# A recurrence whose candidate is summed by one scan in PSUM, and a transformer block whose norms are made tile by tile

## The reference

```
x = x + topk_mask(fside, cond, x)
x = x + small_attention(x, cond)
x = x + gru(cond, x)          # 512 steps, state 4 x 512
x = x + dit_block(x, cond)    # per batch of 4

def cell(h, x):
    gi = x @ W_ih + b_ih;  gh = h @ W_hh + b_hh
    r = sigmoid(i_r + h_r);  z = sigmoid(i_z + h_z)
    n = tanh(i_n + r * h_n)
    return (1 - z) * n + z * h

def dit_block(x, c):
    shift1, scale1, gate1, shift2, scale2, gate2 = split(c @ ada_w + ada_b)
    x1 = ln(x) * (1 + scale1) + shift1
    x = x + gate1 * (attention(x1) @ out_w + out_b)      # 16 heads of 128
    x2 = ln(x) * (1 + scale2) + shift2
    return x + gate2 * (gelu(x2 @ w1 + b1) @ w2 + b2)    # hidden 2048
```

## Time and profile before

| | |
|---|---|
| median of 3 runs | 4443.78 us (4442.07 to 4444.65) |
| the profiled execution | 4447.41 us, span 4445.7 us |
| TensorE busy | 3784.4 us (85%), 69948 matmuls |
| weight loads | 2814.5 us (63%) |
| VectorE busy | 2845.6 us (64%) |
| ScalarE busy | 2080.4 us (47%) |
| GpSimd busy | 517.7 us (12%) |

### The profile page before, as it was taken

One profiled execution on the slowest core, in us unless ns is written; L12 is line 12 of the kernel. 1 busy time (PEld: TensorE's weight loads), 2 busy tenths in 40 slices (PEclk: granted clock), 3 DMA queues, 4 the chain that ended last, 5 costly groups with the idle time before them and its releaser, 6 DMA issues. The chain is left out here.

```text
span 4445.7 us, 180216 instructions
## 1 busy us (share of the span) xinstructions
PE 3784.4 (85%) x69948; PEld 2814.5 (63%) x69948; DVE 2845.6 (64%) x11557; ACT 2080.4 (47%) x7520; POOL 517.7 (12%) x425
## 2 busy tenths in 40 slices
PE   1526766776999999999999996998799889988997
PEld 1424453543489999999999993564356436633653
DVE  7877787786677777777777773574267226623752
ACT  2015574665755555555555551453145215422532
POOL 3005374471000000000000000001000100010001
PEclk9999998998955555555555557999899989998999
DMA  2002131232000000000000006110221122022102
GB/s 85 0 24 67 49 115 40 77 98 69 0 6 6 6 6 6 6 6 6 6 6 6 6 6 238 67 38 38 109 76 29 62 106 65 20 80 114 46 12 85
DMA packets 114616, 209.71 MB, mean 47 GB/s; under 512 B 44154, under 2 KB 76922, under 8 KB 112000
## 3 DMA queue, kind: packets, MB, share of 16 engines
q1 hardware_dynamic: 114436, 207.35, 13.7%
HBM read 165.35 MB, written 33.57 MB: 45 GB/s over the span
## 5 line engine op out<-in xcount | busy, mean ns | idle before, releaser
L497 ACT ACTIVATE dit_prob<-dit_bank,dit_head_nbias 128x512 f32<-128x512 f32 x256 | 176.0, 688 | 350.7 <-DVE dit_head_nbias L515 350.3
L1272 PE MATMUL gru_sum_na<-gru_state_parts,w_hh_lo 128*128 128x4 f16 x4096 | 263.3, 169 | 0.0
L1406 DVE TENSOR_TENSOR_SCAN gru_state_parts<-gru_keep_gate,gru_new_and_old 128x24 f16<-128x24 f32 x1024 | 213.1, 208 | 71.4
L1282 PE MATMUL gru_sum_na<-gru_state_parts,w_hh_hi 128*128 128x8 f16 x4096 | 254.1, 168 | 0.0
L1282 PE MATMUL gru_sum_ra<-gru_state_parts,w_hh_hi 128*128 128x8 f16 x4096 | 254.1, 168 | 0.0
L1282 PE MATMUL gru_sum_za<-gru_state_parts,w_hh_hi 128*128 128x8 f16 x4096 | 254.1, 168 | 0.0
L1272 PE MATMUL gru_sum_nb<-gru_state_parts,w_hh_lo 128*128 128x4 f16 x4096 | 252.1, 166 | 0.0
L1272 PE MATMUL gru_sum_za<-gru_state_parts,w_hh_lo 128*128 128x4 f16 x4096 | 252.1, 166 | 0.0
L1272 PE MATMUL gru_sum_rb<-gru_state_parts,w_hh_lo 128*128 128x4 f16 x4096 | 252.1, 166 | 0.0
L1272 PE MATMUL gru_sum_ra<-gru_state_parts,w_hh_lo 128*128 128x4 f16 x4096 | 252.1, 166 | 0.0
L1272 PE MATMUL gru_sum_zb<-gru_state_parts,w_hh_lo 128*128 128x4 f16 x4096 | 252.1, 166 | 0.0
(11 more groups left out here) (311 smaller groups left out, 13415.8 us busy)
## 6 DMA issues: line engine op xcount, KB each, us to landing
dit_w_qk<-w_qk_parts SPq DMA_DIRECT2D x64, 512.0 KB, 3.6
weights<-w_parts SPq DMA_DIRECT2D x8, 4096.0 KB, 12.2
weights<-w_out_parts SPq DMA_DIRECT2D x5, 4096.0 KB, 17.6
weights<-w_v_parts SPq DMA_DIRECT2D x5, 4096.0 KB, 13.3
small_given_w<-in_L_cond_qkv_w SPq DMA_DIRECT2D x48, 256.0 KB, 3.1
w_qk_parts<-small_parts_w SPq DMA_DIRECT2D x32, 256.0 KB, 2.1
small_given_w<-in_L_cond_ffn_w SPq DMA_DIRECT2D x32, 256.0 KB, 3.3
w_parts<-small_parts_w SPq DMA_DIRECT2D x32, 256.0 KB, 2.5
```

The costliest lines, as they stand in the source:

```text
L497: act.activation(self.prob[:, t % 2, :], self.S[t % 2], ACT.Exp, bias=bias[:, t:t + 1], scale=self.scale, accum_out=self.rsum[:, t:t + 1]) ...
L1272: mm = pe.matmul(bank[:, j * 2 * B:j * 2 * B + B], w_hh[1][:, k, c:c + P], parts[:, par, 0, k, :, LAST], start=opens, stop=False, skip_gro ...
L1282: mm = pe.matmul(bank[:, j * 2 * B:(j + 1) * 2 * B].rearrange("p (e b) -> p e b", e=2), w_hh[0][:, k, c:c + P], parts[:, par, :, k, :, LAS ...
L1406: return dve.tensor_tensor_scan(line(out), line(factor), line(term), 0.0, ALU.mult, ALU.add)
```

## The change

In the recurrence:

- The candidate's products are written in PSUM into an array `sum_n` of two banks for each of two alternating steps. An element has four slots: high and low column (0, 1), bias (2, filled once), the input's term (3, which ScalarE now copies there for the next step, between the keep gate and the tanh). The two totals of na and nb and `candidate` go; the candidate's scan reads the four slots in PSUM (32 elements in place of 24), with factors 0, 1, 1, r.
- The matmuls of a step stand in another order, and the order of a few of VectorE's steps differs too.
- NOW is 4: TensorE's loop body holds 8 steps, pieces of `gi_now` hold 4.

In the last block:

- x is loaded into a buffer of its own (`given_x`), for the next batch during the attention of this one. The next batch's first norm (`normed_rows`) stands on VectorE ahead of the MLP's second half, its 16 transposes behind that half's first tile, and the modulation behind that tile's addition.
- GpSimd adds the attention's gated bias to x at the batch's start. VectorE gates, adds and norms each tile right behind its out-projection (`add_attention`). The tile's four transposes (`turn_tile`) stand in the middle of the next tile's projection, those of tile 3 between the MLP's second and third hidden block.
- The first four hidden blocks of the MLP are summed over 384 columns first (tiles 0 to 2) and then over the last 128.
- The heads' turned outputs lie in V's space, the MLP's second half is written out (no loop), and so is the fourth batch.

```diff
 def gru_phase
-        NOW = 2
+        NOW = 4
-        LAST = 2
+        LAST, GATED = 2, 3
-        reset = m.sb("reset_gate", [P, KD, B, 3])
-        cand = m.sb("candidate", [P, 2, KD, B, 3])
-        n_in = m.sb("n_in", [P, KD, B, 3])
+        reset = m.sb("reset_gate", [P, KD, B, 4])
+        n_in = m.sb("n_in", [P, KD, B, 4])
+        n_banks = m.ps("sum_n", [P, 2, 2, 4 * P])
+        n_terms = n_banks[:, :, :, 0:HALF * B * 4].rearrange("p v h (f b s) -> p v h f b s", b=B, s=4)
...
         TensorE
                     pe.wait_ge(hi_a, i + 1)
-                    pe.wait_ge(u_a, i + 1)
-                    low(na_bank, N_GATE, first, first, par, opens=True)
-                    low(rb_bank, R_GATE, second, first, par)
-                    low(zb_bank, Z_GATE, second, first, par)
-                    pe.wait_ge(u_b, i + 1)
-                    low(nb_bank, N_GATE, second, first, par, opens=True)
-                    low(ra_bank, R_GATE, first, first, par)
-                    low(za_bank, Z_GATE, first, first, par)
+                    low(rb, R_GATE, second, first, par)
+                    low(za, Z_GATE, first, first, par)
+                    low(ra, R_GATE, first, first, par)
+                    low(zb, Z_GATE, second, first, par)
+                    pe.wait_ge(gn_ready, i + 1)
+                    low(na, N_GATE, first, first, par, opens=True)
                     pe.wait_ge(lo_a, i + 1)
...
                     pe.wait_ge(hi_b, i + 1)
-                    low(za_bank, Z_GATE, first, second, par)
-                    low(na_bank, N_GATE, first, second, par)
-                    low(ra_bank, R_GATE, first, second, par)
+                    low(ra, R_GATE, first, second, par)
+                    high(zb, Z_GATE, second, first, par)
+                    low(za, Z_GATE, first, second, par)
                     pe.wait_ge(lo_b, i + 1)
+                    high(ra, R_GATE, first, second, par).then_inc(ra_sum, 1)
+                    high(na, N_GATE, first, second, par)
+                    high(za, Z_GATE, first, second, par).then_inc(za_sum, 1)
+                    low(rb, R_GATE, second, second, par)
+                    low(na, N_GATE, first, second, par).then_inc(na_sum, 1)
...
         ScalarE
-                    act.activation(cand[:, par, :, :, LAST], gi_n[:, at(i)].rearrange("p o f b -> p (o f) b"), ACT.Copy)\
-                       .then_inc(gn_ready, 1)
...
                     act.activation(keep[:, A, :, LAST], z_in[:, A], ACT.Sigmoid, scale=-1.0 / GS).then_inc(keep_a, 1)
+                    copy_gi_n(i + 1, 1 - par)
                     act.wait_ge(n_in_a, i + 1)
...
         VectorE
+                    dve.wait_ge(r_a, i + 1)
                     dve.wait_ge(na_sum, i + 1)
-                    total(cand[:, par, A, :, 0], na_bank).then_inc(u_a, 1)
-                    dve.wait_ge(r_a, i + 2)
-                    dve.wait_ge(u_a, i + 2)
-                    dve.wait_ge(gn_ready, i + 2)
-                    chain(n_in[:, A], reset[:, A], cand[:, par, A]).then_inc(n_in_a, 1)
+                    chain(n_in[:, A], reset[:, A], n_terms[:, par, 0]).then_inc(n_in_a, 1)
...
 def dit_phase
         TensorE
+                for t in range(1, TT):
+                    if t + 1 < TT:
+                        turn_heads(t + 1)
+                    project_out(t, low_heads)
+                    turn_tile(t - 1)
+                    project_out(t, high_heads)
...
+                early = (TT - 1) * P
+                pe.wait_ge(tile_yl, b * TT + TT - 1)
+                for j in range(4):
...
+                    hidden(j, j, 0, early)
+                    if j == 1:
+                        turn_tile(TT - 1)
+                pe.wait_ge(tile_yl, b * TT + TT)
+                for j in range(4):
+                    hidden(j, j, early, T).then_inc(hid_sum, 1)
...
+                    mm.then_inc(mlp_sum, 1)
+                    if t == 0 and more:
+                        turn_rows(b + 1)
...
+            with pe.Fori(0, B - 1) as b:
+                batch(b, True)
+            batch(B - 1, False)
...
         VectorE
+                def add_attention(t):
+                    n = b * TT + t
+                    dve.wait_ge(att_sum, n + 1)
...
+                    dve.scalar_tensor_tensor(out=A[:, t, :], in0=work[t % 2][:], scalar=UNSCALE, in1=gates[:, 0, :],
+                                             op0=ALU.mult, op1=ALU.mult).then_inc(att_gated, 1)
...
+                    dve.tensor_tensor(A[:, t, :], A[:, t, :], X[:, t, :], ALU.add).then_inc(a_ready, 1)
...
+                    dve.bn_stats(stats2[:, t, :], A[:, t, :]).then_inc(stats2_ready, 1)
...
+                    dve.reciprocal(rstd2[:, t:t + 1], rstd2[:, t:t + 1]).then_inc(rstd2_ready, 1)
...
+                    dve.tensor_scalar(xn[:, t, :], A[:, t, :], mv2[:, t, 0:1], rstd2[:, t:t + 1], ALU.subtract,
+                                      ALU.mult).then_inc(xn2_ready, 1)
```

More of the change, by code:

```diff
@@ L1334, in _ @@
+                    low(nb, N_GATE, second, second, par)
+                    high(nb, N_GATE, second, first, par)
+                    low(nb, N_GATE, second, first, par).then_inc(nb_sum, 1)
             pe.wait_ge(kept, T)
@@ L1763, in _ @@
[L1763 to L1773 removed]
+                        hidden(g * 4 + j, j, 0, T).then_inc(hid_sum, 1)
@@ L1827, in _ @@
                            .then_inc(hh_ready, 1)
+                if more:
+                    parts_of_rows(b + 1)
+            with act.Fori(0, B - 1) as b:
+                batch(b, True)
+            batch(B - 1, False)
         @block.vector
```

377 lines of the change are left out of this document (224 added, 153 removed).

## The result

| | before | after |
|---|---|---|
| median | 4443.97 us (4442.07 to 4444.65, 4 runs) | 4534.55 us (4528.09 to 4538.60, 4 runs) |
| profiled execution, span | 4447.41 us, 4445.7 us | 4528.09 us, 4526.3 us |
| recurrence (first load of its loop to first transpose behind it) | 1447.9 us | 1670.4 us |
| last block (first load of x to the end) | 1696.1 us | 1559.4 us |

The change makes the kernel slower by 2.0%: ratio 1.0203, 95% interval 1.0186 to 1.0221. The forecast was 4268 us in a range of 4230 to 4322. The two lower lines say where to look: the last block gave 137 us, as forecast, and the recurrence, from which 38 us were to come, took 222 us more.

The account below looks back on a forecast made before the run. A loop through three engines bounds the recurrence (TensorE waits 0.16 us a step); two long TensorE waits a batch burden the last block. Gains 38+70+70−2 = 176 us from 4447.4 give 4271 profiled, median 4268; range 4230 to 4322.

Parts of the forecast that it names:

- the code rival: TensorE's doubled recurrence loop isn't kept on the engine; each of 64 back edges waits for code: 218 us, 4486; chance 0.04.
- (a): Recurrence: new matmul order puts 12 groups of four, not 13, ahead of ra's last sum: 0.107 us less a step.
- (b): Recurrence: candidate's total goes; its scan reads 32 elements from PSUM, 0.018 us longer, PSUM source free, start about as before.
- R: Time mark within a recurrence step: the start of the last matmul of ra's sum, from which later events are counted.
- (c): Recurrence: ScalarE's copy of the input term moves ahead of the tanh, which starts at R+0.97 instead of R+0.93: 0.04 us later.
- The back edge: TensorE's recurrence loop: jumping back costs 0.13 us, formerly hidden in the wait; now 0.05 us shows once in eight steps.
- (e): Last block, between batches: early load and norm of x cut TensorE's lost 25.9 us by 23.2, three times: 70 us.
- (f): Last block, between out-projection and MLP: norms covered by matmuls cut the lost 19.8 us by 17.5, four times: 70 us.
- the rival of short covers: Last block: VectorE is late behind every tile, with scaling passes at 1339 ns: 31 us lost, 4299; chance 0.10.
- (g): Last block: next x queued ahead of the third head's weights in three batches costs 2 us in sum.

Follow-up runs that it names:

- six-step kernel: The changed kernel with a TensorE loop of six steps (600 matmuls) and pieces of three: 4274.30 us, ratio 0.9615.
- four-step kernel: The changed kernel with a TensorE loop of four steps (400 matmuls) and gi_now pieces of two: 4287.84 us, ratio 0.9648.

## Why the prediction was wrong

**The step that failed** is the price and the chance of the code rival. The prediction read the empty instruction queue rightly, a body of 400 matmuls is kept, and worked out what it would mean if one of 800 were not: 4486 us, slower. Then it gave that 0.04, because the new body's 1650 instructions are fewer than 2048. That bound is the Trainium skill's ("Runtime: NRT & Kernel Launch", Instruction fetch mechanics), and no row of before stood behind it at this length. The runs show that this comparison doesn't hold: whether a body of 1612 is kept depends on where it starts (4295 us with 128 instructions ahead of it, 4535 with none, 4542 with 256), and the changed kernel has it in a bad place. Nothing in the trace of before could tell 800 from 400; the two rules pulled apart, and one of them was taken for the answer. A mechanism of that weight, undecided by any row, should have had a large share of the chance and pulled the range's upper end up to it.

**Its size.** Two packets at 1.7 us an edge, 3.4 by 64, were 218 us. The size is near and the mechanism isn't. Measured: not two packets at each edge but nine at nearly every second, 208 us by 30, some 7 us a pair of waits, and the small gaps behind: 1670.4 less the 1410.9 of the same loop well placed is 259 us. The forecast of 4271 for a profiled execution and 259 make 4530; it took 4528.1, and the median lies 6.5 above it.

**(a) The order** was priced at 0.107 us a step, 55 us; it is worth 32, because the scan behind it starts later. **(b) The scan from PSUM** takes 221 ns (forecast 226, with PSUM as a source at nothing) and begins 0.03 late; the 0.065 us that the fixed cycles of the Trainium skill ("VectorE: DVE Perf Modes", the TRN2 errata) would add are not in it. (By the prediction's own terms they would have moved the tanh from R+0.97 to about R+1.00 and cost some 13 us, not 20.) **(c) The copy ahead of the tanh** does come 0.11 before it, but costs nothing: with the copy behind the tanh the time is the same. The 0.02 net at the tanh came from the scan's later start. (a) to (c) were off singly and right in sum: a step of 2.75 us. **The back edge**: with eight well placed steps 1410.9/512 is 2.756 us, the forecast to 0.001. With six (85 edges) it is 1.2 us more in all, with four (128) another 7.0: an edge costs between 0.06 and 0.16 us. The recurrence without fetching thus gives 36 to 37 us, forecast 38.

**(e) and (f), the last block.** 1696.1 less 1559.4 is 137 us, in the six-step kernel 135; forecast 138. Between batches 1.3 us stand where 0.95 were forecast; the fourth tiles wait 1.0 us in the four batches, 0.25 each, where 0.4 were forecast. The scaling passes run at 546 ns (L2010), so the rival of short covers had no ground. **(g)** The third head's weights: 0.48, 0.32 and 0.16 us in three batches here, but 1.63, 1.12 and 1.67 in the four-step kernel. The forecast's 2 us in sum lies between 1.0 and 4.4. What it didn't foresee is the clock's dip between the MLP's halves, up to 1.7 us a batch.

**What beats both.** The changed kernel with six steps a turn and the load of x behind the first pair of heads: 4272.70 us, ratio 0.9614 of before and 5 us from the forecast. By the arithmetic of pieces, an estimate, 1210 instructions touch six at most wherever they start and 1420 seven (one place was run for each); 1612 touch seven from 181 of the 256 starts within a piece and eight from the other 75, so eight steps are good only in a place that the next edit ahead of the loop can move.

## What to carry over

An unrolled loop is code that must fit: before a loop body is made longer, see whether the instruction queue is empty inside it, and when it is, don't take that for proof about twice the length. Whether a body of 1612 instructions is kept here depends on its start, so an unrelated edit far ahead may cost or give 6% of this kernel; keep the body clearly shorter, and when a trace shows packets of the instruction queue in a loop with waits for "issue" at its back edge, shorten the body before anything else is judged by the time. A change of three parts is read part by part: here 174 us of gain were hidden under 259 of loss from one number.

## What the runs showed of the hardware

- TensorE's loops of some 810, 1210 and 1420 instructions moved no instruction packets from 1400 to 2600 us; one of 1612 moved six at its start and none behind in two places (256 instructions apart), and 277 and 286 in the recurrence in two others.
- A badly placed loop of eight steps isn't fetched at every turn but at nearly every second, nine packets each time, with a turn of 22 us between that has no packet and no wait inside; one of sixteen steps is fetched at every turn. Two instructions more (1614) made it 15 times in 64, at irregular distances. Neither was expected, and why it is so stays open; no run tried it.
- A fetch isn't the 1.7 us of a small load: 4.3 to 5.0 us at the edge, 1.9 to 2.5 in the step behind it.
- A fulfilled wait on TensorE costs time too: 256 of them, 128 instructions, made the loop start 18 us later than in the changed kernel, 512 made it 30 and 768 made it 45, some 15 us for each 256.
- A scan of 32 elements with one source in PSUM takes 221 ns, one of 24 from SBUF 208.
- The granted clock fell to 0.5 for 3.4 us behind a TensorE wait of 2.58 us between the MLP's halves in four batches of one run and in one batch of another; eight matmuls of 512 columns then started 0.43 us apart in place of 0.22.
